# Graph layers on one core: one gathered tile of every even step of layer 1 goes from GpSimd to SP, row by row, by byte offsets

## What is computed

```python
h = relu(layernorm(x));  x = x + gcn(h)              # layer 0
h = relu(layernorm(x))
for l in range(2):                                   # the kernel's layers 1 and 2
    seg  = dst * 65 + edge_type
    agg  = segment_sum(h[src], seg);  cnt = segment_sum(1, seg)
    conv = einsum('nrd,rdk->nk', agg / max(cnt, 1), W[l]) + h @ root[l] + bias[l]
    h    = relu(conv) + relu(h @ res_W[l] + res_b[l])
x = x + h
```

## Time and profile before

| | us |
|---|---|
| median of 3 runs | 10409.57 |
| lowest and highest | 10406.67, 10411.6 |
| the profiled execution's own time | 10414.85 |
| its span, first to last instruction | 10412.8 |
| POOL busy | 7664.3 |
| DVE busy | 5439.9 |
| PE busy | 4552.2 |
| ACT busy | 2260.0 |
| mean granted TensorE clock | 0.654 |

### The profile page before, as it was taken

The page is one execution under the profiler, slowest core; times in us unless marked ns, Lnnn a source line. Parts: engine busy times, 40 slices in busy tenths (PEclk is TensorE's granted clock), DMA queues, the critical chain, the costliest instruction groups (busy, mean ns, idle before and its releaser), DMA issues.

```text
span 10412.8 us, 180513 instructions
## 1 busy us (share of the span) xinstructions
PE 4552.2 (44%) x39273; PEld 3351.5 (32%) x39273; DVE 5439.9 (52%) x20234; ACT 2260.0 (22%) x5671; POOL 7664.3 (74%) x8196
## 2 busy tenths in 40 slices
PE   4489898885444444444444444222222222222222
PEld 3366666663222222222222222122222222222222
DVE  9877676766766766766776776222222222222222
ACT  7756565652111111111111111000000000000000
POOL 6577777775777777777777776777777777777777
PEclk8889999996666666666666666555555555555555
DMA  3234444445444444444444444111111111111112
GB/s 88 60 129 147 139 147 140 146 138 166 147 146 138 146 142 142 146 141 144 142 143 145 140 144 146 30 30 30 30 30 30 30 30 30 30 30 30 30 30 41
DMA packets 517848, 1018.14 MB, mean 98 GB/s; under 512 B 224773, under 2 KB 270869, under 8 KB 516309
## 3 DMA queue, kind: packets, MB, share of 16 engines
q1 hardware_dynamic: 242628, 745.04, 19.6%
q0 software_dynamic: 254784, 263.18, 13.0%
q10 hardware_dynamic: 19600, 1.66, 0.1%
HBM read 559.40 MB, written 454.23 MB: 97 GB/s over the span
## 4 chain that ended last, share of the span: by engine, by line
POOL 60%; issue 23%; PE 8%; DVE 4%; SPq 2%; ACT 1%; DMA 1%; POOLq 0%; ACTq 0%; DVEq 0%
POOL rows L878 33%; POOL w_parts L878 27%; PE y_ps L1241 3%; PE block_ps L1328 2%; DVE ystage L1569 2%; SPq L309 1%; PE sums_ps L1293 1%; PE y_ps L1320 1%; ACT scr L1016 1%; SPq L305 0%; PE signs_ps L1320 0%; DMA y_table<-ystage 0%; ACTq L309 0%; DVE onehot L1604 0%; DMA rows<-h_table,idx_st 0%
## 5 line engine op out<-in xcount | busy, mean ns | idle before, releaser
L878 POOL DMA_INDIRECT rows<-y_table,idx_st x3185 | 3009.1, 945 | 1052.4 <-issue 1051.8
L878 POOL DMA_INDIRECT w_parts<-y_table,idx_st x3163 | 2986.9, 944 | 964.5 <-issue 964.5
L1675 DVE TENSOR_SCALAR rr<-rr 128x64 f32<-128x64 f32 x198 | 43.4, 219 | 4125.0 <-PE block_ps L1270 4125.0
L1436 PE MATMUL sums_ps<-onehot,rows 128*64 128x64 f32 x6468 | 762.2, 315 | 2669.9 <-DMA rows<-y_table,idx_st 2537.8
L1436 PE MATMUL sums_ps<-w_parts 128*64 128x64 f32 x6424 | 754.6, 315 | 2583.7 <-DMA w_parts<-y_table,idx_st 2505.4
L878 POOL DMA_INDIRECT rows<-h_table,idx_st x1452 | 1399.0, 964 | 552.6 <-issue 453.5
L1436 PEld LDWEIGHTS sums_ps<-onehot,rows 128*64 128x64 f32 x6468 | 710.7, 225 | 2748.8 <-issue 1320.4
L1436 PEld LDWEIGHTS sums_ps<-w_parts 128*64 128x64 f32 x6424 | 707.4, 225 | 2658.0 <-issue 2169.1
L982 ACT ACTIVATE idx_st<-edges 128x11 int32 (+1 forms) x720 | 141.3, 210 | 5850.9 <-PE sums_ps L1436 3218.2
L1006 ACT ACTIVATE ystage<-y_ps 128x512 f32<-128x512 f32 (+1 forms) x1782 | 1010.7, 568 | 977.5 <-PE y_ps L1241 819.6
L1614 DVE TENSOR_SCALAR_CACHE_REDUCE w_raw<-edges,step_key 128x384 bf16<-128x384 f32 x1568 | 850.8, 606 | 15.6 <-DVE step_key L1594 15.6
(11 more groups left out here) (230 smaller groups left out, 6414.8 us busy)
## 6 DMA issues: line engine op xcount, KB each, us to landing
y_table<-ystage SPq DMA_DIRECT2D x396, 768.0 KB, 3.7
edges<-key_row SPq DMA_DIRECT2D x198, 832.0 KB, 6.3
y_table<-ystage SPq DMA_DIRECT2D x198, 608.0 KB, 3.3
w_parts<-y_table ACTq DMA_DIRECT2D x6272, 0.2 KB
rows<-y_table SPq DMA_DIRECT2D x6272, 0.2 KB
w_raw<-key_row SPq DMA_DIRECT2D x99, 832.0 KB, 7.1
rows<-y_table,idx_st POOLq DMA_INDIRECT x3185
w_parts<-y_table,idx_st POOLq DMA_INDIRECT x3163, 2.5
```

The costliest lines, as they stand in the source:

```text
L878: pool.indirect_dma_start(out=rows_of(l, u)[:, j, k, 0:D], out_offset=None, in_=table, in_offset=bass.IndirectOffsetOnAxis(ap=idx_of(l, u, ...
L1436: ins = nc.tensor.matmul(sums_ps[u][0:width, c:c + W], rows_of(l, u)[:, j, k, 0:width], onehot_of(l, u)[:, j, k, :], start=False, stop=False)
```

## The change

In layer 1, tile 10 of group 0 of every even step is no longer gathered by POOL; SP loads it, 128 rows in four bursts of 32 over two steps, and all 128 rows of step 0 ahead of the loop. Odd steps of layer 1 are unchanged. In layer 2, SP's 64 rows a step come in two bursts of 32 rather than four of 16. In both layers and on both engines the rows are addressed by byte offsets in a view of the table as bytes: ACT multiplies a tile's 128 indices by 256 in one instruction (`place_rows`), and the loader loads the products into registers. SP's first two y saves now stand together, and the third key load in front of the second burst. Its index load comes first in the even step, now in layer 1 too, where key loads follow it.

```diff
+    ROW_BYTES = 4 * D
...
-        row_idx = [extra[0:1, u * P:(u + 1) * P] for u in range(2)]
+        row_idx = [extra[0:1, n * P:(n + 1) * P] for n in range(2)]
+        row_at = [extra[0:1, (2 + n) * P:(3 + n) * P] for n in range(2)]
+        y_bytes = [t.rearrange("(o n) d -> o (n d)", o=1).bitcast(u8) for t in y_table]
+
+        def by_rows(l, u):
+            return l == ROW_LAYER or l == 1 and u == 0
...
-            return [k for k in range(tiles) if not (l == ROW_LAYER and j == 0 and k == ROW_K)]
+            return [k for k in range(tiles) if not (by_rows(l, u) and j == 0 and k == ROW_K)]
...
+        def place_rows(n, loaded):
+            wait_alone(nc.scalar, row_idx_loaded[n], loaded * 16)
+            nc.scalar.activation(row_at[n], row_idx[n], ACT.Copy, scale=float(ROW_BYTES))\
+              .then_inc(row_placed[n], 1)
...
-                    row_idx[u][:, c0:c0 + ROW_BATCH], engines=[which], min_val=0, max_val=NBK * P * RX - 1,
+                    row_at[n][:, c0:c0 + ROW_BATCH], engines=[which], min_val=0,
+                    max_val=(NBK * P * RX - 1) * ROW_BYTES,
...
-                    eng.dma_start(rows_of(l, u)[r:r + 1, 0, ROW_K, 0:D], y_table[l - 1][bass.ds(value, 1), :])\
-                       .then_inc(rows_landed[u], 16)
+                    eng.dma_start(rows_of(l, u)[r:r + 1, 0, k, 0:D].bitcast(u8),
+                                  y_bytes[l - 1][:, bass.ds(value, ROW_BYTES)]).then_inc(rows_landed[l][n], 16)
...
-                    if l == ROW_LAYER:
-                        wait_alone(sp, agg_done[l], 1)
-                        load_row_idx(sp, 0, 0)
-                        wait_alone(sp, row_idx_loaded[0], 16)
-                        load_rows(sp, mybir.EngineType.SP, l, 0, 0, P)
+                    loads = (l - 1) * (S // 2) + 1
+                    per_step = 64 if l == 1 else ROW_HALF
+                    wait_alone(sp, agg_done[l], 1)
+                    load_row_idx(sp, 0, 0, 0)
+                    wait_alone(sp, row_placed[0], loads)
+                    load_rows(sp, mybir.EngineType.SP, l, 0, 0, 2 * per_step)
...
-                                load_rows(sp, mybir.EngineType.SP, l, 0, u * ROW_HALF + n * ROW_BATCH, ROW_BATCH)
+                                load_rows(sp, mybir.EngineType.SP, l, 0, u * per_step + n * (per_step // 2), per_step // 2)
...
                         if more and u == 0:
                             wait_alone(sp, agg_done[l], s * J + 2 * J + 1)
-                            wait_alone(sp, row_idx_loaded[0], i * 16 + 32)
+                            wait_alone(sp, row_placed[0], i + loads + 1)
                         next_rows(0)
                         if l < 2:
-                            save_y(l, s, u, (0,))
+                            save_y(l, s, u, range(YG - 1))
+                        if l == 1:
+                            next_keys(2)
                         next_rows(1)
                         if l < 2:
-                            save_y(l, s, u, (1,))
-                        next_rows(2)
-                        if l == 1:
-                            next_keys(2)
-                        if l < 2:
                             save_y(l, s, u, (YG - 1,))
-                        next_rows(3)
...
-                            sp_step(i, u, l == ROW_LAYER)
+                            sp_step(i, u, True)
...
                         read_sums(l, s, 1 - u)
+                        if u == 0 and more:
+                            place_rows(0, i + loads + 1)
+                            if l == ROW_LAYER:
+                                load_row_idx(act, 1, i + 1, 1)
                         stage_ahead(0)
...
                         if l == ROW_LAYER and u == 0 and more:
-                            load_row_idx(act, i + 1, 1)
+                            place_rows(1, i + 2)
+                            wait_alone(act, row_placed[1], i + 2)
...
-                                if l == ROW_LAYER and j == 0 and k == ROW_K:
-                                    pe.wait_ge(rows_landed[u], i * (16 * P) + 16 * P)
+                                if by_rows(l, u) and j == 0 and k == ROW_K:
+                                    pe.wait_ge(rows_landed[l][u], i * (16 * P) + 16 * P)
```

More of the change, by code:

```diff
@@ L47, in gnn_kernel @@
                tile_base, iota_row, part_col, ident_in, step_diff, out):
[L51 removed]
+    f32, bf16, i32, u8 = mybir.dt.float32, mybir.dt.bfloat16, mybir.dt.int32, mybir.dt.uint8
     ALU, ACT, AX = mybir.AluOpType, mybir.ActivationFunctionType, mybir.AxisListType
@@ L303, in load_rows, with pool_tiles @@
-        def load_rows(eng, which, l, u, r0, n):
-            for c0 in range(r0, r0 + n, ROW_BATCH):
+        row_idx = [extra[0:1, n * P:(n + 1) * P] for n in range(2)]
[3 more added lines that the diff above has]
+            return l == ROW_LAYER or l == 1 and u == 0
+        def pool_tiles(l, u, j, tiles):
+            return [k for k in range(tiles) if not (by_rows(l, u) and j == 0 and k == ROW_K)]
@@ new lines, in load_row_idx @@
+        def load_row_idx(eng, n, pair, u, k=ROW_K):
+            at = (pair * 2 + u) * T + k
+            eng.dma_start(row_idx[n].rearrange("p (e a) -> p e a", a=1),
+                          col_table[1:2, :, bass.ds(at, 1)], allow_slow_non_contiguous=True)\
+               .then_inc(row_idx_loaded[n], 16)
+        def place_rows(n, loaded):
+            wait_alone(nc.scalar, row_idx_loaded[n], loaded * 16)
+            nc.scalar.activation(row_at[n], row_idx[n], ACT.Copy, scale=float(ROW_BYTES))\
+              .then_inc(row_placed[n], 1)
@@ L305, in load_rows @@
+        def load_rows(eng, which, l, n, r0, rows, k=ROW_K):
+            u = min(n, 1)
+            for c0 in range(r0, r0 + rows, ROW_BATCH):
                 _, values = nc.values_load_multi_w_load_instructions(
-                    row_idx[u][:, c0:c0 + ROW_BATCH], engines=[which], min_val=0, max_val=NBK * P * RX - 1,
+                    row_at[n][:, c0:c0 + ROW_BATCH], engines=[which], min_val=0,
+                    max_val=(NBK * P * RX - 1) * ROW_BYTES,
                     skip_runtime_bounds_check_because="sources are clamped to the table, types lie below R")
@@ L411, in gnn_kernel @@
         gathered = [[[sem(f"gathered{l}{u}{j}") for j in range(J)] for u in range(2)] for l in range(3)]
-        rows_landed = [sem(f"rows_landed{u}") for u in range(2)]
-        row_idx_loaded = [sem(f"row_idx_loaded{u}") for u in range(2)]
+        rows_landed = [None] + [[sem(f"rows_landed{l}{n}") for n in range(l)] for l in (1, 2)]
+        row_idx_loaded = [sem(f"row_idx_loaded{n}") for n in range(2)]
+        row_placed = [sem(f"row_placed{n}") for n in range(2)]
         idx_staged = [sem(f"idx_staged{l}") for l in range(3)]
@@ L876, in gather_group @@
                         wait_alone(pool, agg_done[l], q + 1)
-                        for k in pool_tiles(l, j, tiles):
+                        for k in pool_tiles(l, u, j, tiles):
                             pool.indirect_dma_start(
@@ L1097, in _ @@
                         nc.scalar.activation(col[:, 3:4], eps[:, :], ACT.Copy).then_inc(y_read[l], 1)
+                    loads = (l - 1) * (S // 2) + 1
+                    place_rows(0, loads)
                     if l == ROW_LAYER:
@@ L1429, in sum_step @@
                             pe.wait_ge(onehot_ready[l], q + 1)
-                            by_pool = len(pool_tiles(l, j, K))
-                            pe.wait_ge(gathered[l][u][j], i * (16 * by_pool) + 16 * len(pool_tiles(l, j, tiles)))
+                            by_pool = len(pool_tiles(l, u, j, K))
+                            pe.wait_ge(gathered[l][u][j], i * (16 * by_pool) + 16 * len(pool_tiles(l, u, j, tiles)))
                             for k in range(tiles):
-                                if l == ROW_LAYER and j == 0 and k == ROW_K:
-                                    pe.wait_ge(rows_landed[u], i * (16 * P) + 16 * P)
+                                if by_rows(l, u) and j == 0 and k == ROW_K:
+                                    pe.wait_ge(rows_landed[l][u], i * (16 * P) + 16 * P)
                                 c = column_of(j * K + k, T, LEFT)
```

16 lines of the change are left out of this document (4 added, 12 removed).

## The result

The changed kernel takes **10352.23 us** (median of five runs, 10345.81 to 10357.54) against 10409.57 for the kernel before on the same chip (five runs, 10406.67 to 10416.28). The ratio is 0.9945, with a 95% interval of 0.9932 to 0.9959. The forecast was 10348.4 us, a ratio of 0.9941, with a range of 10342 to 10364. The profiled execution took 10357.54 us, its span 10355.6.

A forecast was written before the change was run, and what follows sets the result against it. The prediction took POOL's gathers, 1.2494 us each, as the bound. Removing 49 in layer 1 saves 61.2 us, all additions costed at zero: from the median 10409.57 to 10348.4 us, range 10342 to 10364.

The forecast's parts named there:

- What binds: Layers 1 and 2: POOL's gathers set the pace, about 1.25 us each, with only "issue" ahead of them.
- the term of the sum: Layer 1, even steps: 49 gathers taken from POOL at 1.2494 us each, 61.2 us less.
- What was costed at zero: Index load and ACT's multiplication in layer 1, and the row loads at layer 1's start: no time added.
- PE's lag: Layer 1: PE may wait a few us for SP's rows, hidden from POOL, which needs that group about 68 us later.
- late keys: Layer 1: key loads behind SP's burst come 2 us late, covered by DVE's 11.3 us idle a step.
- the chain's length at the old price: SP's row chain in layer 1 at 0.489 us a row: 73.4 us a pair against POOL's 81.2.
- the upper end of the row's price: SP's row loads: 0.489 us a row, the old price from layer 2, taken for the forecast.
- rival 4: SP and ACT: the cheaper address saves up to 0.19 us a row where nobody waits, changing no time; no chance given.
- the 67.6 us: Layer 2's start: SP's chain of rows running free, between PE's waits at 6564.80 and 6632.38, taken as its time a pair.
- The lower bound of the row's price: SP's row loads: 225 ns issue plus a sixteenth of a 1.23 us register load, 0.30 us a row.
- Rival 1: SP's row loads: a dearer byte-form issue, 105 ns more a row, makes them the bound, 10670 us; chance 0.05.
- Rivals 2 and 3: No change, about 10410, another engine or late transfer holding the pair, 0.03; a stall at layer 1's start, 10359, 0.06.

The follow-up runs named there:

- experiment 2: The changed kernel with layer 1's tile back on POOL, layer 2's byte offsets and the new order kept: 10437.41 us against 10437.43 for the kernel before.
- Experiment 1: The changed kernel with row numbers for byte offsets, SP and ACT multiplying each again: 10554.43 us (one execution) against 10412.01 for the kernel before.

## Why the prediction was right, and where it was not

**What binds, and the term of the sum: right.** Layer 1 lost 49 gathers at 1.2494 us forecast, 61.2; measured 60.6. POOL's pace held at 1.2496 us, with "issue" ahead of all gathers, and experiment 2 shows that nothing else contributed.

**What was costed at zero: right.** The gap to layer 2 is 27.3 us (forecast 27), layer 2 takes 3902.6 us against 3903.9, and at layer 1's start the rows ended at 2506.0 (forecast near 2512) and PE ended its wait at 2507 (forecast near 2514), with POOL due there at 2530.0, by 2448.79 + 65 × 1.2496. PE's lag was hidden as argued. The forecast had the index there before ACT asked for it, with 10 us against the 3.6 that it needs. That was wrong: ACT waits 6.7 us a pair for it, since SP's index load now stands behind the second burst and the third save. The zero held because this lies inside the 10.7 that ACT had stood for PE. Its product takes 0.31 us, not 0.2. DVE still waits for PE, 791.5 / 74 = 10.7 us a step (11.3 before), so late keys were covered.

**The step that failed: the chain's length at the old price.** I wrote "73.4 us against POOL's 81.2. It holds, with 7.8 us to spare, or 61 ns a row", took the upper end of the row's price because "nothing in the forecast needs the lower", and held in rival 4 that the cheaper address "changes no time". Experiment 1 measured that very case at 84.7 us a pair. The sum was 11.3 us short. Three things were missing.

First, the 67.6 us that I took from layer 2 were its first pair, in which SP's loop does not yet return. The next wait of PE for SP's rows, which I did not read, stands 69.9 us behind the second, and the one after it 70.3:

```profile
6702.32 0.48 PE L1436 MATMUL sums_ps<-onehot,rows 128*64 128x64 f32 x2 [27.34 <-DMA rows<-y_table]
```

The kernel with row numbers has the same in layer 1: its first pair takes 80.2 us, nearly the 80.1 that its own forecast had, and the next two 84.2 and 84.3, as each of these holds a return of the loop at 3.7 to 3.9 us.

```profile
2519.51 0.48 PE L1451 MATMUL sums_ps<-onehot,rows 128*64 128x64 f32 x2 [53.76 <-DMA rows<-y_table]
2599.74 0.48 PE L1451 MATMUL sums_ps<-onehot,rows 128*64 128x64 f32 x2 [13.55 <-DMA rows<-y_table]
```

Second, two register loads a pair stand behind a key load, which layer 2 doesn't have, and take 3.7 us in place of 1.23: 4.9 us. Third, the issues of saves and key loads between the bursts take 7.2 us by themselves, where I had added 5.8 with their gaps; of the 11.3 us some 2.5 are left for them and the gaps. The waits of ACT and PE are what the long chain does to them and no part of it, for SP itself waited 0.2 us in 3000.

With the true chain the old price loses: 10554 us in one execution, 1.4% more than before. The threshold was no 61 ns above 0.489 us but, as an estimate from 84.7 − 81.2 = 3.5 us over 128 rows, and with the loop's code fetched as in that run, 27 ns below it. The new price, 0.397, lies 92 ns below, and with the branch that now costs 0.24 us the chain is 69.3 us and the margin 12.

So the number came out right for a reason that the text had set aside, and the 0.86 that it gave the forecast rested on a margin that was not there at the price it took. That the real price was the lower one was luck for the sum. The lower bound of the row's price (0.30 us) and the upper (0.489) gave different signs, and the choice between them was the real question of this change. I missed it because my sum for the worse end seemed to fit.

**The rivals.** Rival 1 (row loads bind) had the right mechanism, with the wrong point of decision; the dear issue that it rested on did not come (228 ns against 225). Rivals 2 and 3 did not happen: DVE's waits are for PE and not for keys, and POOL did not stall at layer 1's start. Taking 49 gathers off POOL's queue gave 0.55%, all of their intervals. The rule set against the rows (the Trainium skill, "DMA: Bandwidth & Descriptors", "Issuing engines are not separate DMA queues") says that issuing from several engines saves only the time to initiate. The trace agrees with that: this time is what was saved. It does not agree that it is small here, at 1.25 us a gather on the engine that is the path. The remaining 3.8 us of the median over the forecast are about the 4 us ahead of layer 1, within the spread of the five runs (12 us).

## What to carry to other kernels

When one engine's issue of gathers is the path, each gather moved elsewhere counts with its full interval, if the queue that takes it can keep up; so price the helper's whole chain, with what stands between its bursts and what its loop costs at the branch, and not the burst alone. A price taken from a stretch without those neighbours is a lower bound: if the sum fits by only a tenth, treat the worse end as undecided. The first turn of a loop is such a stretch too: take the price from a later one, which holds the loop's return. And a chain that is longer than the bound's pays twice, in each round and again at the layer's end, while one that is shorter pays nothing even after a start 42 us late.

## What the runs showed of the hardware that I had not expected

- **Loops whose code is fetched again in every turn.** The page's line of the code queue went from 662 packets before to 145 after:

```profile
q14 instruction: 145, 1.19, 0.0%
```

  Before, 55 of them fell in 400 us of layer 2, where SP's and ACT's loops were 409 and 423 instructions long, and each turn stood 2.4 to 2.6 us at the branch. After, with 333 and 281 on SP and 300 on ACT, there were none, and the branch took 0.2 us. With row numbers in layer 1 SP's loop has 461 and stands 3.7 to 3.9 us at each return. Length alone does not decide: in the kernel of experiment 2 a loop of 281 was fetched again, at 2.4 to 2.6 us a turn. The Trainium skill, "Runtime: NRT & Kernel Launch", section "Instruction fetch mechanics", says that a taken branch whose target lies outside the window of code already present forces a fetch. The trace agrees that the stall stands at the branch; which loops stay in, no run here settles.
- **Register loads.** 16 registers take 1.23 us, but 2.3 to 3.4 behind the issue of an 832 KB key load in the changed kernel and 3.2 to 3.8 in the one with row numbers. 32 take 2.0 to 2.2 us, 3.2 to 4.3 behind a key load, and 3.6 to 5.5 on ACT behind its copies of y.
- **Chips that differ.** The same kernel took 10410 to 10440 us on some and 14826 to 14934 on others, whose sequencers have pauses of some 0.7 us. A version's worth is not the same on both: the one of experiment 2, with the tile on POOL, is 2.4% faster than the kernel before on those and equal on the others. Why these chips pause was not found.
